# Graph attention on one core: the score products' third runs regrouped over pairs of units

## The chip, the cores and the metric

The kernel runs on one core of one Trainium2 chip. Its time is device microseconds (us) of one execution; the number quoted is the median of several. TensorE (PE, with its weight loads as PEld), VectorE (DVE), ScalarE (ACT), GpSimd (POOL) and SyncE (SP) each run their own queue in order and meet at semaphores.

## The reference, cut to what matters

Two layers, each a graph layer and a mixture of experts, over 1250 nodes of 512 features and 20000 edges. The change is in the first graph layer, an attention with 8 heads of 64 over the edges:

```python
qkv = x @ W
q, k, v = jnp.split(qkv, [Fqk, 2 * Fqk], axis=-1)
aw = jnp.einsum('ehf,ehf->eh', q[src] * scaling, k[dest])
e = jnp.exp(aw - m[src])            # m: maximum over the edges of a source
alpha = e / denom[src]
out = segment_sum(alpha[:, :, None] * v[dest], src)
x = x + out
```

The kernel computes it densely: for each source node the products with all 1250 nodes, plus the logarithm of the number of edges between the two (very negative where there is none), then a softmax over the row.

## The kernel before, in words

The attention runs over 40 units (`UNITS`): 10 tiles of 125 source nodes (`i = u // 4`) times 4 pairs of heads (`j = u % 4`). The order of the work is written out by hand for each engine; semaphores carry counts. For a unit u:

- **Scores** (PE, `scores`, L687; matmul at L696). The 1250 columns are cut in three thirds (`KPIECES`). For each third there is one product for each of the two heads, on rows 0 to 63 and on rows 64 to 127 of the array. Thirds have a running number `g = 3 * u + t`, and third g writes the PSUM bank `2 * h + g % 2`. So it waits until third g - 2 has been taken out (`z_made`).
- **Negated scores** (DVE, `negate_scores`, L1930; L1945). One instruction for a third and head takes the product from PSUM, adds the logarithms, negates, writes `SC[u % 2]`, and carries the minimum along in `neg_max`. The thirds t = 1, 2 read the running minimum; t = 0 starts it. Before t = 0 it waits until the weights of unit u - 2 have been turned.
- **Exponential** (ACT, L1242), one of 1250 columns for each head, when all thirds of the head are there.
- **Turned weights** (PE, `turn_weights`, L699; L707): 20 transposes in 5 blocks of 4. ACT moves blocks 0, 1, 3 from PSUM (L1249), DVE blocks 2 and 4 (`move_block`, L1949; L1952). Three banks take turns as a ring, and a block waits for the move of the block three places back (`release_ring`).
- **Weighed values** (PE, `weigh_values`, L711; L725): 20 products on 64 columns of the array each (40 records), one unit late, into bank 7. ACT moves the result (L1265), PE turns it back a unit later (`turn_output`, L734), and DVE adds it to X (`add_output`, L1966; L1973), which counts `x_added`.

`weigh_values` begins with these waits:

```python
def weigh_values(u):
    above_zero(pe, S("ot_moved"), u)
    above_zero(pe, S("x_added"), 2 * u)
    if tile_at(u + 1, LOGITS_AT) is not None:
        pe.wait_ge(S("log_taken"), tile_at(u + 1, LOGITS_AT) + 1)
```

In unit u PE calls `weigh_values(u - 1)`; the wait is then for `add_output(u - 2)`, which DVE does in unit u behind the negated scores of that unit's first run and its first block move, and PE's part of which (`turn_output(u - 2)`) stands between blocks 2 and 3.

Other work is spread over the units. Row statistics (DVE) in units 5, 9, 13, ...; a normalised row tile turned on PE (L752) in units 6, 10, ...; the routing logits (`route_tile`, PE L762; taken by DVE at L1987) in units 7, 11, ..., 39; ranks (L769, DVE L2002) in units 8, 12, ...; and `out_degree` (DVE, L2079) at the end of the even units 12 to 30. In units 36, 37 and 38 DVE has chains of short instructions (`early_counts`, `early_owners`, `early_done`).

Of the kernel before, what the change touches and what calls it, by code (L numbers as in the profile page):

```python
# [61 lines left out]
UNITS = T * PAIRS  # L62
# [21 lines left out]
def tile_at(u, first):  # L84

    i = (u - first) // PAIRS
    return i if u >= first and (u - first) % PAIRS == 0 and i < T else None


def above_zero(eng, sem, value):  # L90

    if not (isinstance(value, int) and value <= 0):
        eng.wait_ge(sem, value)


def gnn_moe_kernel(nc, x, src, dst, L0_gnn_W, L0_ffn_gate_w, L0_ffn_w1, L0_ffn_w2, L0_ffn_w3,
# [7 lines left out]
    with ExitStack() as ctx:  # L104
# [129 lines left out]
        def bank(b, rows=128, cols=512, off=0):  # L234
            return ps[0:rows, 512 * b + off:512 * b + off + cols]
# [43 lines left out]
        def S(n):  # L279
            return s[n]  # L280
# [230 lines left out]
        def _(pe):  # L511
# [175 lines left out]
            def scores(u, thirds):  # L687

                i, j = u // PAIRS, u % PAIRS
                for t in thirds:  # L690
                    a, z = KPIECES[t]
                    g = 3 * u + t
                    for h in range(2):
                        r = DH * h
                        above_zero(pe, S("z_made"), 2 * (g - 2) + h + 1 if g > 1 else 0)
                        pe.matmul(bank(2 * h + g % 2, P, z - a), QT[r:r + DH, i, j, :],  # L696
                                  KT[r:r + DH, j, a:z], start=True, stop=True).then_inc(S("s_made"), 1)

            def turn_weights(u, blocks):  # L699

                for b in blocks:
                    n = ring_at(u, b)
                    release_ring(n - 3)
                    for k in range(4):
                        h, kt = (4 * b + k) // T, (4 * b + k) % T
                        pe.wait_ge(S("p_made"), 2 * u + h + 1)
                        ins = pe.transpose(bank(4 + n % 3, P, P, k * P), SC[u % 2][h][:, kt * P:kt * P + P],  # L707
                                           ident[0:P, 0:P])
                    ins.then_inc(S("p_turned"), 1)
# [20 lines left out]
            def turn_output(u):  # L730

                pe.wait_ge(S("ot_moved"), u + 1)
                above_zero(pe, S("x_added"), 2 * u)
                pe.transpose(bank(7, P, 128, 256), OT[u % 2], ident[:, :]).then_inc(S("ot_turned"), 1)  # L734
# [6 lines left out]
            def output_bank_free(u):  # L741

                pe.wait_ge(S("ot_moved"), min(u + 1, UNITS))
                pe.wait_ge(S("x_added"), 2 * min(u, UNITS))

            def turn_normed_row(i):

                n = RING_AT[("row", i)]
                release_ring(n - 3)
                pe.wait_ge(S("xn_made"), T + i + 1)  # L750
                for c in range(C):
                    ins = pe.transpose(bank(4 + n % 3, 128, P, c * P), XR[i % 3][:, c * 128:c * 128 + 128],  # L752
                                       ident[0:P, 0:P])
                ins.then_inc(S("xt_turned"), 1)

            def route_tile(i):

                if i == 0:
                    pe.wait_ge(S("gate_in"), 16)
                pe.wait_ge(S("xt_moved"), T + i + 1)  # L760
                for c in range(C):
                    ins = pe.matmul(bank(7, P, E0, 128), XT[:, c, i * P:i * P + P], gate_w[:, c, 0:E0],  # L762
                                    start=c == 0, stop=c == C - 1, skip_group_check=True)
                ins.then_inc(S("log_made"), 1)

            def rank_tile(i):

                pe.wait_ge(S("mask_made"), i + 1)
                pe.matmul(bank(7, 126, 8, 136), before[0:126, 0:126], counted[:, i % 2, :], start=True, stop=True,  # L769
                          skip_group_check=True).then_inc(S("rank_made"), 1)  # L770

            def take_out_counts(k):

                pe.matmul(bank(7, 1, 8, 144), ident[0:126, 125:126], counted[:, k, :], start=True, stop=True,
                          skip_group_check=True).then_inc(S("count_made"), 1)

            for u in range(UNITS):
                if u + 1 < UNITS:
                    scores(u + 1, (0, 1))
                if tile_at(u, LOGITS_AT) is not None:  # L780
                    output_bank_free(u - 2)
                    route_tile(tile_at(u, LOGITS_AT))
                if tile_at(u, RANKS_AT) is not None:
                    output_bank_free(u - 2)
                    rank_tile(tile_at(u, RANKS_AT))
                    if tile_at(u, RANKS_AT) == EARLY_ROWS:
                        take_out_counts(EARLY_ROWS % 2)
                turn_weights(u, range(0, 3))
                if 2 <= u:
                    turn_output(u - 2)  # L790
                turn_weights(u, range(3, BLOCKS))
                if tile_at(u, ROWS_AT) is not None:
                    turn_normed_row(tile_at(u, ROWS_AT))
                if u + 1 < UNITS:
                    scores(u + 1, (2,))
                if 1 <= u:
                    weigh_values(u - 1)

# [923 lines left out]
        def _(dve):  # L1722
# [207 lines left out]
            def negate_scores(u, t):  # L1930

                i, j = u // PAIRS, u % PAIRS
                a, z = KPIECES[t]
                g = 3 * u + t
                if t == 0:
                    if j == 0:
                        dve.wait_ge(logs_in[i % 2], 32 * (i // 2) + 32)
                    above_zero(dve, S("p_turned"), BLOCKS * (u - 1))
                    above_zero(dve, S("rden_made"), 2 * (u - 1))
                for h in range(2):  # L1940
                    dve.wait_ge(S("s_made"), 2 * g + h + 1)
                    least = neg_max[:, 2 * (u % 2) + h:2 * (u % 2) + h + 1]
                    if t:
                        dve.wait_ge(S("z_made"), 2 * (g - 1) + h + 1)
                    dve.tensor_tensor_reduce(SC[u % 2][h][:, a:z], bank(2 * h + g % 2, P, z - a), LNB[i % 2][:, a:z],  # L1945
                                             -1.0, least if t else 3.0e38, ALU.add, ALU.min, least)\
                       .then_inc(S("z_made"), 1)

            def move_block(u, b):  # L1949
                dve.wait_ge(S("p_turned"), BLOCKS * u + b + 1)  # L1950
                above_zero(dve, S("o_made"), u - 1)
                dve.tensor_copy(PT[u % 2][:, 4 * b:4 * b + 4, :],  # L1952
                                bank(4 + ring_at(u, b) % 3, P, 4 * P).rearrange("p (i n) -> p i n", n=P))\
                   .then_inc(S("pt_moved_v"), 1)
# [130 lines left out]
                negate_scores(0, t)  # L2085
            for u in range(UNITS):
                if u + 1 < UNITS:
                    negate_scores(u + 1, 0)
                    negate_scores(u + 1, 1)
                move_block(u, DVE_BLOCKS[0])  # L2090
                if 2 <= u:
                    add_output(u - 2)
                if tile_at(u, LOGITS_AT) is not None:
                    take_logits(tile_at(u, LOGITS_AT))
                if tile_at(u, RANKS_AT) is not None:
                    take_ranks(tile_at(u, RANKS_AT))
                if tile_at(u, STATS_AT) is not None:
                    dve.wait_ge(S("x_added"), 2 * (u - 1))
                    row_stats(X, tile_at(u, STATS_AT))
                inverse_den(u)  # L2100
                if u + 1 < UNITS:
                    negate_scores(u + 1, 2)
                move_block(u, DVE_BLOCKS[1])
                if tile_at(u, STATS_AT) is not None:
                    normed_row(tile_at(u, STATS_AT))
                if tile_at(u, LOGITS_AT) is not None:
                    pick_two(tile_at(u, LOGITS_AT))
                if u >= OUT_DEGREE_AT and u % 2 == 0 and u < OUT_DEGREE_AT + 2 * T:
                    out_degree((u - OUT_DEGREE_AT) // 2)
                if u == RANKS_AT + PAIRS * EARLY_ROWS:  # L2110
                    early_counts()
                if u == RANKS_AT + PAIRS * EARLY_ROWS + 1:
                    early_owners(EARLY_TILES, early_owner, S("slot_made"))
                if u == RANKS_AT + PAIRS * EARLY_ROWS + 2:
                    early_done(EARLY_TILES)
# [414 lines left out]
```

## Time and profile before

| | |
|---|---|
| time, median of 3 | 880.06 us (879.31 to 882.21) |
| time of the profiled execution | 882.13 us |
| its span | 880.4 us |
| PE busy in the span | 828.3 us (94%) |
| attention's units | from 183.60 to about 490 us of the span |

Times in the rows are microseconds from the start of the span, and durations in microseconds unless marked ns. A row of the timeline gives start, duration, engine, line, operation, what is written and read, how many records it merges, and in brackets the idle time of the engine before it and what ended it. A matmul with float32 operands leaves two records.

### The profile page before, as it was taken

The numbers are of one execution on the slowest core, as the hardware profiler recorded it, in microseconds if no ns is written. First come the engines' busy times: TensorE is split into PE (matmuls) and PEld (weight loads), VectorE is DVE, ScalarE is ACT, GpSimd is POOL, SyncE is SP. The second block draws the span as 40 slices with busy tenths as digits, with TensorE's granted clock in tenths as the row PEclk, the third lists the DMA queues.
The fourth block names the chain that finished last, engine by engine and source line by source line (L and its number), as shares of the span: only waits on it lengthen the run. The fifth ranks groups of instructions, "written<-read, shape, count | busy, mean of one in ns | idle before, by whom it ended". The sixth has DMA issues, their size and how long they took to land.

```text
span 880.4 us, 16072 instructions
## 1 busy us (share of the span) xinstructions
PE 828.3 (94%) x5125; PEld 559.6 (64%) x5125; DVE 560.4 (64%) x1839; ACT 374.3 (43%) x680; POOL 207.9 (24%) x381
## 2 busy tenths in 40 slices
PE   5999999899999999999999899999979999996996
PEld 2456555357777777777777676777644445766664
DVE  6489999167878888888877365555552515875111
ACT  1344544366665666666566233343310021543331
POOL 4200000000022022102203342122255511564453
PEclk9999999999999999999999899999999999996999
DMA  9918878896102223110825636554136250185450
GB/s 253 339 29 218 219 203 222 153 320 173 31 25 73 67 80 85 33 51 25 294 95 148 212 96 197 171 168 149 61 108 146 75 179 13 36 265 147 147 173 18
DMA packets 87362, 121.00 MB, mean 137 GB/s; under 512 B 40781, under 2 KB 50157, under 8 KB 87021
## 3 DMA queue, kind: packets, MB, share of 16 engines
q1 hardware_dynamic: 73677, 101.82, 39.7%
q0 software_dynamic: 13600, 18.11, 7.4%
q8 instruction: 46, 0.75, 0.4%
q14 instruction: 39, 0.32, 0.1%
HBM read 65.52 MB, written 57.08 MB: 139 GB/s over the span
## 4 chain that ended last, share of the span: by engine, by line
PE 75%; DVE 9%; DMA 7%; issue 3%; POOL 2%; ACT 2%; SPq 1%; DVEq 0%; POOLq 0%; ACTq 0%
PE ps L806 18%; PE ps L696 11%; PE ps L725 10%; PE ps L707 10%; PE ps L936 7%; PE ps L586 5%; PE ps L963 4%; PE ps L813 4%; DVE R_B L1844 3%; PE ps L591 2%; DVE R_B L1843 2%; DMA R_A<-slots_d 1%; DMA R_B<-slots_d,slot 1%; PE ps L527 1%; DMA R_A<-slots_d,slot 1%
## 5 line engine op out<-in xcount | busy, mean ns | idle before, releaser
L806 PE MATMUL ps<-R_B,R_A 128*128 x612 | 185.7, 446 | 1.7 <-ACT R_A L1418 0.6
L806 PEld LDWEIGHTS ps<-R_B,R_A 128*128 128x128 f32 x612 | 112.0, 194 | 34.8 <-issue 24.5
L1242 ACT ACTIVATE R_A<-R_A,neg_max 125x1250 f32<-125x1250 f32 x80 | 106.6, 1333 | 57.5 <-DVE neg_max L1945 57.5
L696 PE MATMUL ps<-R_B 64*125 64x417 f32 (+1 forms) x480 | 106.5, 544 | 2.5 <-ACT XN L1184 1.5
L1945 DVE CUSTOM_DVE_ANT_0 R_A<-ps,R_B,neg_max 125x417 f32<-125x417 f32 (+1 forms) x160 | 97.6, 648 | 15.0 <-PE ps L696 15.0
L707 PEld LDWEIGHTS ps<-ident,R_A 125*125 125x125 f32 x800 | 93.7, 188 | 14.2 <-issue 13.3
L707 PE MATMUL ps<-ident,R_A 125*125 125x125 f32 x800 | 102.3, 277 | 0.0
L725 PEld LDWEIGHTS ps<-R_W,XN 125*64 125x64 f32 x1600 | 85.3, 136 | 23.6 <-issue 23.6
L725 PE MATMUL ps<-R_W,XN 125*64 125x125 f32 x1600 | 94.7, 272 | 0.5 <-DVE X L1973 0.5
L1249 ACT ACTIVATE R_W<-ps 125x500 f32<-125x500 f32 x120 | 66.1, 585 | 47.8 <-PE ps L707 47.8
L586 PE MATMUL ps<-XT,R_W 128*128 128x500 f32 (+1 forms) x192 | 72.4, 522 | 0.6 <-ACT XT L1167 0.6
L1945 DVE CUSTOM_DVE_ANT_0 R_A<-ps,R_B 125x417 f32<-125x417 f32 x80 | 44.2, 590 | 44.7 <-PE ps L696 31.2
L1844 DVE TENSOR_SCALAR R_B<-R_B 125x418 bf16<-125x418 uint16 x180 | 69.2, 384 | 0.0
L813 PEld LDWEIGHTS ps<-ident,R_A 128*128 128x128 f32 x306 | 38.7, 143 | 34.5 <-issue 20.3
L1952 DVE COPY R_W<-ps 125x500 f32<-125x500 f32 x80 | 54.0, 675 | 9.0 <-PE ps L707 8.7
L696 PEld LDWEIGHTS ps<-R_B 64*125 64x125 f32 x480 | 39.6, 183 | 30.1 <-issue 21.6
L813 PE MATMUL ps<-ident,R_A 128*128 128x128 f32 x306 | 49.9, 279 | 7.5 <-DMA R_A<-slots_d 3.6
L1578 POOL TENSOR_TENSOR rms<-ssum,half_pow 128x1 f32<-128x1 f32 x54 | 30.0, 557 | 102.5 <-DVE ssum L2125 67.8
L1843 DVE TENSOR_SCALAR R_B<-R_B 125x125 bf16<-125x125 uint16 x180 | 45.1, 250 | 13.6 <-PE ps L527 13.2
L586 PEld LDWEIGHTS ps<-XT,R_W 128*128 128x128 f32 x192 | 36.9, 196 | 25.4 <-issue 23.7
L527 PE MATMUL ps<-R_B 125*125 125x418 bf16 x180 | 43.6, 351 | 6.8 <-DVE R_B L1844 5.0
L1554 POOL IOTA R_B<- 125x4 int32 x2 | 0.3, 148 | 196.3 <-DVE mv L1752 196.3
(272 smaller groups left out, 1151.0 us busy)
## 6 DMA issues: line engine op xcount, KB each, us to landing
slots_d<-R_B SPq DMA_DIRECT2D x9, 2322.0 KB, 12.2
R_B<-in_L_ffn_w_dram SPq DMA_DIRECT2D x28, 512.0 KB, 6.8
R_A<-slots_d SPq DMA_DIRECT2D x27, 256.0 KB, 2.8
slots_d<-R_A SPq DMA_DIRECT2D x27, 256.0 KB, 2.5
counts_d<-R_A SPq DMA_DIRECT2D x10, 546.9 KB
logs_d<-R_B SPq DMA_DIRECT2D x10, 546.9 KB
R_B<-logs_d SPq DMA_DIRECT2D x10, 546.9 KB
R_B<-counts_d SPq DMA_DIRECT2D x10, 546.9 KB
```

What stands on the lines that cost most here:

```text
L586: ins = pe.matmul(b[:, 0:z - a], Wqkv[:, c, w:w + 128], XT[:, c, a:z], start=c == 0, stop=c == C - 1)
L696: pe.matmul(bank(2 * h + g % 2, P, z - a), QT[r:r + DH, i, j, :], KT[r:r + DH, j, a:z], start=True, stop=True).then_inc(S("s_made"), 1)
L707: ins = pe.transpose(bank(4 + n % 3, P, P, k * P), SC[u % 2][h][:, kt * P:kt * P + P], ident[0:P, 0:P])
L725: ins = pe.matmul(ps[r:r + DH, 512 * 7:512 * 7 + P], XN[:, kt, (2 * j + h) * DH:(2 * j + h) * DH + DH], PT[u % 2][:, T * h + kt, :], start ...
L806: ins = pe.matmul(bank(b, TM, width), lhs[:, c * TM:c * TM + TM], flat[:, bass.ds(e * (n * width) + c * width, width)], start=c == 0, stop ...
L813: ins = pe.transpose(bank(b, 128, TM, c * TM), source[:, c * 128:c * 128 + 128], ident[:, :])
L936: return pe.matmul(bank(b, 128, z - a), HS[i][:, c * 128:c * 128 + 128], counts_of[i][:, a:z], start=i == 0, stop=i == T - 1)
L1242: act.activation(SC[u % 2][h], SC[u % 2][h], ACT.Exp, bias=neg_max[:, 2 * (u % 2) + h:2 * (u % 2) + h + 1], scale=-1.0, accum_out=den[:, 2 ...
L1249: act.activation(PT[u % 2][:, 4 * b:4 * b + 4, :], bank(4 + ring_at(u, b) % 3, P, 4 * P).rearrange("p (i n) -> p i n", n=P), ACT.Copy).the ...
L1843: dve.tensor_scalar(oh_dst[:, slot, :], iota_dst, win[:, 0, w:w + 1], None, ALU.is_equal)
L1844: return dve.tensor_scalar(hot_of[:, slot, 0:width], iota_src[:, 0:width], win[:, 1, w:w + 1], win[:, 2, w:w + 1], ALU.is_equal, ALU.mult)
L1945: dve.tensor_tensor_reduce(SC[u % 2][h][:, a:z], bank(2 * h + g % 2, P, z - a), LNB[i % 2][:, a:z], -1.0, least if t else 3.0e38, ALU.add, ...
```

## The change

Every unit had two score runs on PE: at its top thirds 0 and 1 of the next unit, and behind its turned weights third 2 of the next unit. Now an even unit u does thirds 0 and 1 of unit u + 1 at its top, and behind its turned weights third 2 of unit u + 1 and third 0 of unit u + 2. An odd unit u does thirds 1 and 2 of unit u + 1 at its top and has no second run. DVE's order follows: in an even unit third 0 of unit u + 2 is negated behind block 4, and in an odd unit nothing is negated between `inverse_den` and block 4. The order of the thirds, and what each waits for, are as before.

```diff
             for u in range(UNITS):
                 if u + 1 < UNITS:
-                    scores(u + 1, (0, 1))
+                    scores(u + 1, (1, 2) if u % 2 else (0, 1))
...
                 turn_weights(u, range(3, BLOCKS))
...
-                if u + 1 < UNITS:
+                if u + 1 < UNITS and u % 2 == 0:
                     scores(u + 1, (2,))
+                if u + 2 < UNITS and u % 2 == 0:
+                    scores(u + 2, (0,))
                 if 1 <= u:
                     weigh_values(u - 1)
...
                 if u + 1 < UNITS:
-                    negate_scores(u + 1, 0)
-                    negate_scores(u + 1, 1)
+                    negate_scores(u + 1, 1 if u % 2 else 0)
+                    negate_scores(u + 1, 2 if u % 2 else 1)
                 move_block(u, DVE_BLOCKS[0])
...
                 inverse_den(u)
-                if u + 1 < UNITS:
+                if u + 1 < UNITS and u % 2 == 0:
                     negate_scores(u + 1, 2)
                 move_block(u, DVE_BLOCKS[1])
+                if u + 2 < UNITS and u % 2 == 0:
+                    negate_scores(u + 2, 0)
```

## Rows read from the trace of the kernel before

**Rows 1.** The page's first part: busy time, share of the span, instructions.
```profile
PE 828.3 (94%) x5125; PEld 559.6 (64%) x5125; DVE 560.4 (64%) x1839; ACT 374.3 (43%) x680; POOL 207.9 (24%) x381
```
**Rows 2.** Chain that ended last, unit 25 of the attention: start, duration, what.
```profile
403.39 1.60 PE ps L696 x8
404.99 1.50 PE ps L707 x12
406.50 0.11 PE ps L734
406.61 0.87 PE ps L707 x8
407.48 0.90 PE ps L696 x4
408.38 2.30 PE ps L725 x39
```
**Rows 3.** Busy time by stretch, unit 25: PE, PEld, DVE, ACT, POOL; clock, DMA share, GB/s at the end.
```profile
403.32:410.60 7.28, 7.28 (x75) 5.47 (x73) 7.02 (x22) 4.29 (x7) 2.22 (x4) 1.00 0.29 73
```
**Rows 4.** Timeline, unit 25: PE's first run and DVE up to the added output.
```profile
403.32 1.67 PE L696 MATMUL ps<-R_B 64*125 64x417 f32 x8
...
404.46 0.59 DVE L1945 CUSTOM_DVE_ANT_0 R_A<-ps,R_B 125x417 f32<-125x417 f32 x1 [0.15 <-PE ps L696]
...
405.49 0.65 DVE L1945 CUSTOM_DVE_ANT_0 R_A<-ps,R_B,neg_max 125x417 f32<-125x417 f32 x1
...
406.64 0.67 DVE L1952 COPY R_W<-ps 125x500 f32<-125x500 f32 x1
...
407.23 0.47 DVE L1973 SCALAR_TENSOR_TENSOR X<-ps,rden,X 125x64 f32<-125x64 f32 x2
```
**Rows 5.** Who waited for the added output, whole span: us, times.
```profile
PE ps L725: 0.5, 1
```
**Rows 6.** Timeline, unit 39, which has no score run in the kernel before.
```profile
482.20 1.39 PEld L707 LDWEIGHTS ps<-ident,R_A 125*125 125x125 f32 x12
...
484.47 0.47 DVE L1973 SCALAR_TENSOR_TENSOR X<-ps,rden,X 125x64 f32<-125x64 f32 x2
484.85 0.16 DVE L1987 COPY R_B<-ps 125x8 f32<-125x8 f32 x1
...
485.22 2.37 PE L725 MATMUL ps<-R_W,XN 125*64 125x125 f32 x40 [0.45 <-DVE X L1973]
```
**Rows 7.** Timeline, the attention's start: DVE's third 2 of unit 1, then PE.
```profile
188.68 0.65 DVE L1945 CUSTOM_DVE_ANT_0 R_A<-ps,R_B,neg_max 125x416 f32<-125x416 f32 x1 [0.93 <-PE ps L696]
...
189.40 0.29 PEld L696 LDWEIGHTS ps<-R_B 64*125 64x125 f32 x2 [0.72 <-DVE neg_max L1945]
...
190.92 1.55 PEld L707 LDWEIGHTS ps<-ident,R_A 125*125 125x125 f32 x12 [0.66 <-DVE R_W L1952]
```
**Rows 8.** Timeline, unit 27, which routes a tile.
```profile
420.89 1.39 PEld L707 LDWEIGHTS ps<-ident,R_A 125*125 125x125 f32 x12
...
424.27 1.81 PEld L725 LDWEIGHTS ps<-R_W,XN 125*64 125x64 f32 x34 [0.60 <-issue]
```
**Rows 9.** Timeline, unit 24, which sums an out degree on DVE.
```profile
400.13 0.97 PE L696 MATMUL ps<-R_B 64*125 64x416 f32 x4
...
401.12 0.65 DVE L1945 CUSTOM_DVE_ANT_0 R_A<-ps,R_B,neg_max 125x416 f32<-125x416 f32 x1 [0.35 <-PE ps L696]
...
402.86 1.44 DVE L2079 TENSOR_REDUCE deg_out<-R_B 125x1 f32<-125x1250 f32 x1
```
**Rows 10.** Timeline, unit 38: PE's first run, DVE's first third, the turned row.
```profile
472.34 1.67 PE L696 MATMUL ps<-R_B 64*125 64x417 f32 x8
...
474.22 0.59 DVE L1945 CUSTOM_DVE_ANT_0 R_A<-ps,R_B 125x417 f32<-125x417 f32 x1
...
477.12 0.65 PE L752 MATMUL ps<-ident,R_B 125*128 125x125 f32 x4 [0.62 <-DVE R_W L1952]
```

## The prediction

> **What bounds the kernel now.** I read the page's busy times first, then the chain that ended last, then the timeline of single units. TensorE is busy for 94% of the span [rows 1]; that only says where to look. The chain shows what sets the pace of the attention: through unit 25 it runs on PE alone, from score products to turned weights, the turned output, the second score run and the weighed values, with no other engine and no wait in it [rows 2]. The period is 1.60 + 1.50 + 0.11 + 0.87 + 0.90 + 2.30 = 7.28 us. PE is busy in all 7.28 us of that stretch, at a granted clock of 1.00 (the 2.4 GHz level), but DVE is busy in 7.02 of them [rows 3]. So PE sets the end, and DVE follows it with little in hand. This is the number to remember: a change that shifts work to or from one side of a wait can make DVE's order the bound though its total is smaller.
>
> **What a score run costs.** A run of two thirds took 1.60 us and a run of one third 0.90 [rows 2]. The difference, 0.70, is a third itself; the rest, 0.20, is paid once a run. Before, units 0 to 38 hold 39 runs of each kind. Afterwards, over units 0 to 37, each pair of units has three runs of two thirds: 4.80 us against 2 x 1.60 + 2 x 0.90 = 5.00. There are 19 such pairs (units 38 and 39 do the same as before), and as many instructions as before on every engine. If nothing else moved, the gain would be 19 x 0.20 = 3.8 us.
>
> The Trainium skill (TensorE: Matmul & The Clock Gate, section Single matmul latency) gives a part of a lone matmul that does not depend on its columns, 166 ns at the full clock. By the rows a run's fixed part is 0.20 us; by the page, taken as that part, it would be an estimate of 19 x 0.166 = 3.2 us instead of 3.8. Both are gains, and neither decides the sign.
>
> **Where the run was, and what it covered.** The even unit gets 0.70 us longer on PE (a third more in its second run). The odd unit loses its second run, 0.90 us, if PE can go straight from the turned weights to the weighed values. It can't, because `weigh_values(u - 1)` waits for `x_added` of `add_output(u - 2)`, which DVE does in the same unit behind four negated scores and a block move. I put both on one scale, from T, the start of the first run.
>
> - PE, before: the turned weights are through at T + 4.09 and the weighed values begin at T + 4.99; the 0.90 between is the second run [rows 2].
> - DVE, before: first negation at T + 1.14, added output from T + 3.91 to T + 4.38 [rows 4]. That is 0.29 us after PE is through with the weights, and nobody notices: in the whole span PE waited for the added output once, for 0.5 us [rows 5].
> - DVE, after: the first product comes no sooner, so the start is again T + 1.14. The four negations are now thirds 1 and 2, all with the running minimum. Such a pair took 406.64 - 405.49 = 1.15 us, the pair of third 0 took 405.49 - 404.46 = 1.03 [rows 4]; so 0.12 more. The added output ends at T + 4.50.
>
> The cover that hid this was the second run itself. The one time that PE waited is unit 39, the one late odd unit without a second run in the kernel before. There the added output started at 484.47, ended at 484.94, and the weighed values began at 485.22, PE having idled 0.45 us for it [rows 6]. That is 0.28 behind DVE's end; between them DVE also took out the logits until 485.01, which this unit waits for too. A plain unit has no such step. The bounds of the way from DVE's end to PE's start are 0.07 us (a product released by a negation: 188.68 + 0.65 to 189.40 [rows 7]) and 0.28. I take 0.18, since the wait is followed by the same further waits of `weigh_values` as in unit 39, less the logits.
>
> **The sum**, on the span, in groups of pairs:
>
> - Plain odd units: 3, 5, 9, 13, ... 37, ten of them (the row statistics stand behind the added output, so they change nothing). Weighed values at T + 4.50 + 0.18 = T + 4.68 against T + 4.99: the odd unit gets 0.31 shorter and the even one 0.70 longer. Net +0.39 each, +3.9. With 0.07 and 0.28 it is +2.8 and +4.9.
> - Odd units with routing: 7, 11, ... 35, eight. There PE has the logits' products before the turned weights, DVE waits for block 2, and unit 39 is the direct precedent: 482.20 to 485.22, 3.02 us from the first turned block to the weighed values [rows 6], against 3.38 in unit 27 [rows 8]. So 0.36 back, 0.70 paid, +0.34 each, +2.7.
> - `out_degree`. In unit 24, DVE went from the second run's start 400.13 to the reduction at 402.86 and needed 1.44 more, until 404.30 [rows 9], just before the next first product at 404.46 [rows 4]. Now 1.03 us of third 0 of unit u + 2 stand ahead of it, while PE's next unit starts only 0.70 later, so DVE is 1.03 - 0.70 - 0.16 = about 0.17 late into the odd unit. That adds to the stall in units 13, 17, 21, 25, 29, and something like it in 37 after the early counts: +1.0. In routing units it disappears, since DVE waits for block 2 there. Where DVE had more in hand it is 0.
> - The first pair. Unit 1 has no `x_added` to wait for, and saves its 0.90. But at the start the runs meet with no weighed values between them, and third 2 of unit 2 waits until third 0 of unit 2 has been negated: from 188.68, two negations (1.15), a move (0.59, as from 406.64 to 407.23 [rows 4]) and two more (1.03) are 191.45, plus 0.07 and its own 0.90 make 192.4, against turned weights at 190.92 [rows 7]. So +1.5 - 0.9, some of it cover for other small waits: +0.5 (0 to 1).
> - Unit 38. DVE enters it late, first third at 474.22, 1.88 behind PE's 472.34 instead of 1.14, and PE waited 0.62 for the bank of the turned row [rows 10]. Unit 37 now has no third 2 to negate (1.15 less on DVE, and PE's stall gives it more time), which takes this wait away: -0.7 to 0; I take -0.7.
>
> Together +3.9 + 2.7 + 1.0 + 0.5 - 0.7 = +7.4 us. ACT is no bound: the exponential of unit u + 1 starts no later against PE's next weights than before (its third 2 is ready earlier in odd units, and in even units PE's longer run gives 0.70 more). The logarithms' loads and the expert weights that SP issues on counts of scores are half a unit nearer to their use, and no wait for them shows after the start. Behind the attention the order is unchanged and passes the delay on.
>
> The profiled execution took 882.13 us with a span of 880.4, so its sum is 889.5; it lies 2.07 above the median of 880.06, and I set the forecast against the median: 887.5 us, 0.84% slower.
>
> **The rivals.**
>
> *The wait is not there in time to matter, and the 0.20 is kept.* Then 880.06 - 3.8 = 876.3. It speaks for it that DVE waits 0.15 for the first product in unit 25 [rows 4] and has 1.15 us less to do in the odd unit. But that work stood behind the added output, not ahead of it, and the start is bound by the product itself. It decides if the added output is through before T + 4.09; with the way to PE it would need 0.6 us less ahead of it. Chance 0.06.
>
> *The run's fixed part doesn't go with the run.* The 0.20 could belong to any change between turned weights and weighed values, paid with or without scores between them. With the stall in place this is hidden inside it, so the forecast stands; without it the result is 880.06 within a microsecond. That, with stalls small enough to cancel the gain, is the case of no difference (under 0.3%, 2.6 us, about what a measurement of this kernel can tell from no change). Chance 0.07.
>
> *VectorE becomes the bound in the even units.* It gets eight negations there, 2 x 1.03 + 2 x 1.15 = 4.4 us, and its moves. If its lateness isn't made good in the odd unit but runs on in the ten pairs with `out_degree`, at a further 0.3 to 0.5 us each, 3 to 5 us come on top: about 892. Against it: the odd unit loses what the even one gains, and each stall of PE is time for DVE. Chance 0.10. The Trainium skill (TensorEngine Tiling, section PSUM Bottleneck) says that tiling speeds up TensorE but not taking the results out of PSUM, and that the copies may become the limit. By the rows here it is the copies' place in the order that does it, and not their sum.
>
> **How the numbers follow.** The forecast (stall at the added output, about +7.4) has 0.77. Its range: 0.07 everywhere, no lateness and no cost at the start give 2.8 + 2.7 - 0.7 = +4.8, 884.9; 0.28, a start of 1.0, lateness in all and unit 38's gain lost give 4.9 + 2.7 + 1.0 + 1.0 = +9.6, 889.7. Some of the third rival and the spread of the runs (0.3%) come on top, so 883.0 to 891.0. Slower: 0.77 + 0.10 = 0.87; same 0.07; faster 0.06.
>
> **What would show it.** In the profile after: in odd units no L696 between L707 and L725, and instead a wait of L725 for DVE's L1973, 18 times, each some 0.4 to 0.6 us; even second runs of 1.60 us; the pair of units 24 and 25 about 0.4 to 0.6 longer than before; the wait of L752 in unit 38 gone. The prediction is wrong if L725 follows L707 in odd units with no wait, if DVE's first negation there comes well before T + 1.14, or if time appears outside the attention.

## The result and the profile after

The changed kernel takes 886.27 us (median of 7, 882.48 to 889.15) against 880.71 (7 runs, 878.95 to 882.21). The ratio is 1.0065, with a 95% interval of 1.0043 to 1.0087: 0.65% slower, some 5.7 us, where 7.4 were forecast. The profiled execution has a span of 887.4 us.

First the page's busy time of the kernel after, to hold against [rows 1].

```profile
PE 828.9 (93%) x5125; PEld 564.4 (64%) x5125; DVE 559.4 (63%) x1839; ACT 373.2 (42%) x680; POOL 209.6 (24%) x381
```

PE has the same instructions and, over the whole span, nearly the same busy time. That hides two things, which the span cut in two shows: the attention (from unit 1's first score run to the start of the weighed values in unit 39), then all behind it. The columns are those of [rows 3]; the first two lines are of the kernel before, the others of the kernel after:

```profile
183.60:485.19 301.59, 300.10 (x2952) 227.63 (x2953) 243.67 (x804) 187.80 (x323) 45.79 (x112) 1.00 0.34 102
485.19:880.40 395.21, 366.32 (x1559) 243.15 (x1559) 182.81 (x543) 112.31 (x236) 148.18 (x225) 0.97 0.43 131
```

```profile
182.73:489.31 306.58, 297.99 (x2952) 229.91 (x2952) 242.33 (x804) 186.71 (x323) 46.06 (x112) 1.00 0.33 99
489.31:887.40 398.09, 369.04 (x1559) 245.65 (x1559) 183.14 (x543) 112.28 (x236) 149.63 (x225) 0.96 0.44 130
```

In the attention PE is busy 2.1 us less, but idle 8.6 us instead of 1.5. Behind it PE is busy 2.7 us more with as many records, at a lower mean clock; that part comes back below.

Where PE waits shows in the chain that ended last, here of units 28 and 29 (start, duration, what), to be held against [rows 2]:

```profile
403.30 1.60 PE ps L696 x8
404.90 2.30 PE ps L725 x40
407.20 1.60 PE ps L696 x8
408.80 1.50 PE ps L707 x12
410.30 0.11 PE ps L734
410.41 0.87 PE ps L707 x8
411.28 0.51 issue
411.80 2.37 PE ps L725 x40
```

A word on the numbers of units. Counted in the trace by the weighed values (L725), the stretches that are called units 24, 25 and 27 in the rows and in the prediction are of units 28, 29 and 31, one tile later. Those are units of the same kinds with the same periods (7.50, 7.28 and 8.15 us before), so no sum changes. From here on units go by this count.

The even unit's second run is now 1.60 us. In the odd unit none stands between the turned weights (through at 411.28, 4.08 after the first run's start) and the weighed values, but a gap of 0.51 does. The chain calls it "issue". A plain odd unit, unit 3, shows on the timeline what ends it (the last field is the idle time before):

```profile
204.36 1.67 PE L696 MATMUL ps<-R_B 64*125 64x417 f32 x8
...
205.36 0.65 DVE L1947 CUSTOM_DVE_ANT_0 R_A<-ps,R_B,neg_max 125x417 f32<-125x417 f32 x1 [1.06 <-PE ps L696]
...
207.66 0.67 DVE L1954 COPY R_W<-ps 125x500 f32<-125x500 f32 x1
...
208.25 0.47 DVE L1975 SCALAR_TENSOR_TENSOR X<-ps,rden,X 125x64 f32<-125x64 f32 x2
...
208.78 2.16 PEld L725 LDWEIGHTS ps<-R_W,XN 125*64 125x64 f32 x40 [0.46 <-issue]
208.81 2.37 PE L725 MATMUL ps<-R_W,XN 125*64 125x125 f32 x40 [0.30 <-issue]
```

The added output ends at 208.72, and the first weights for the weighed values are loaded at 208.78. The list of waits of the kernel after gives the same stall two names (us in total, times, longest); together they are 18 times, once for each odd unit from 3 to 37, and 7.4 us:

```profile
PE ps L725 <- issue: 4.2, 10, 0.5
...
PE ps L725 <- DVE X L1975: 3.2, 8, 0.4
```

To compare units, I take the period of unit u as the time from the start of the weighed values (first weight load of L725) in unit u - 1 to that in unit u. In us, with the kernels of the experiments beside it:

| period of | before | after | e1 | e2 | e3 | e4 | e5 | e9 |
|---|---|---|---|---|---|---|---|---|
| 3 (plain odd) | 7.28 | 6.72 | 6.39 | 7.28 | 7.31 | 7.33 | 6.72 | 6.38 |
| 4 (plain even) | 7.28 | 8.01 | 7.98 | 7.28 | 8.01 | 7.31 | 8.01 | 8.37 |
| 13 (odd behind an out degree) | 7.28 | 6.94 | 6.38 | 7.29 | 7.53 | 7.32 | 6.72 | 6.39 |
| 27 (odd with routing) | 8.15 | 7.69 | 7.26 | 8.16 | 8.28 | 8.28 | 7.69 | 7.26 |
| 28 (even, ranks) | 7.50 | 8.24 | 8.20 | 7.50 | 8.23 | 7.53 | 8.23 | 8.59 |
| 14 (even, turned row) | 7.81 | 8.54 | 8.51 | 7.81 | 8.54 | 7.84 | 8.77 | 8.80 |
| 38 | 8.55 | 8.15 | 8.56 | 8.44 | 8.16 | 9.10 | 8.16 | 7.93 |

From unit 3 on the units of a kind agree within 0.05 us in each kernel, but for units 35 to 38, which have work of their own, unit 24 of e4 (7.62), and in e5 units 6, 10 and 34, which turn a row with no out degree ahead of it (8.54, where 14 has 8.77). This grain is far finer than the times of whole executions, which spread over some us.

### The profile page after: what moved, and what is told of

The parts are those of the page before. It is cut to its first block, busy times and chain, and to the rows that moved or that the text cites. A ratio compares the mean times of both kernels' runs of the same rounds, so it can differ in the third digit from the quotient of the medians.

```text
span 887.4 us, 16071 instructions
## 1 busy us (share of the span) xinstructions
PE 828.9 (93%) x5125; PEld 564.4 (64%) x5125; DVE 559.4 (63%) x1839; ACT 373.2 (42%) x680; POOL 209.6 (24%) x381
## 4 chain that ended last, share of the span: by engine, by line
PE 73%; DVE 10%; DMA 7%; issue 4%; POOL 2%; ACT 2%; SPq 1%; DVEq 0%; POOLq 0%; ACTq 0%
PE ps L808 18%; PE ps L696 10%; PE ps L725 10%; PE ps L707 9%; PE ps L938 6%; PE ps L586 5%; PE ps L965 4%; PE ps L815 4%; DVE R_B L1846 3%; PE ps L591 2%; DVE R_B L1845 2%; DMA R_A<-slots_d 2%; PE ps L527 1%; DMA R_B<-slots_d,slot 1%; DMA R_A<-slots_d,slot 1%
## 5 line engine op out<-in xcount | busy, mean ns | idle before, releaser
L696 PE MATMUL ps<-R_B 64*125 64x417 f32 (+1 forms) x480 | 102.2, 536 | 1.7 <-ACT XN L1186 1.5
L725 PE MATMUL ps<-R_W,XN 125*64 125x125 f32 x1600 | 94.8, 272 | 7.9 <-issue 4.2
L725 PEld LDWEIGHTS ps<-R_W,XN 125*64 125x64 f32 x1600 | 85.8, 136 | 22.6 <-issue 22.5
L696 PEld LDWEIGHTS ps<-R_B 64*125 64x125 f32 x480 | 41.5, 183 | 33.6 <-issue 24.4
```

The lines of the kernel that those rows point to most:

```text
L725: ins = pe.matmul(ps[r:r + DH, 512 * 7:512 * 7 + P], XN[:, kt, (2 * j + h) * DH:(2 * j + h) * DH + DH], PT[u % 2][:, T * h + kt, :], start ...
```

## The experiments

### e1: the added output ahead of the block move

```diff
-                move_block(u, DVE_BLOCKS[0])
+                if u % 2 == 0:
+                    move_block(u, DVE_BLOCKS[0])
                 if 2 <= u:
                     add_output(u - 2)
                 if tile_at(u, LOGITS_AT) is not None:
                     take_logits(tile_at(u, LOGITS_AT))
+                if u % 2:
+                    move_block(u, DVE_BLOCKS[0])
```

> The changed kernel, but in odd units DVE adds the output (and takes the logits) before it moves block 2, so x_added comes 0.59 us sooner; the same instructions, one place earlier. Theory A (the gain is lost in the wait for the added output, set by what stands ahead of it on DVE): added output from about T + 3.4 to T + 3.9 after the first run's start, before the turned weights are through at T + 4.09, so L725 follows L707 without a wait in odd units. Odd periods go from 6.72 (6.94 after an out degree, 7.69 with routing) to about 6.38 (6.38, 7.25): 4 x 0.34 + 6 x 0.55 + 8 x 0.44 = 8.2 us faster than the changed kernel, 3 us faster than the kernel before. Theory B (the run's fixed 0.20 us belongs to the switch from turned weights to weighed values and stays): odd periods no shorter than about 6.58, and the kernel before is only just reached. Theory C (DVE's amount of work is the bound): no different from the changed kernel.

Measured: 0.9958 of the kernel before (0.9936 to 0.9980), so faster than both kernels. The timeline of its unit 3:

```profile
203.90 1.67 PE L696 MATMUL ps<-R_B 64*125 64x417 f32 x8
...
207.22 0.48 DVE L1975 SCALAR_TENSOR_TENSOR X<-ps,rden,X 125x64 f32<-125x64 f32 x2
207.62 0.67 DVE L1954 COPY R_W<-ps 125x500 f32<-125x500 f32 x1
...
207.99 1.06 PEld L725 LDWEIGHTS ps<-R_W,XN 125*64 125x64 f32 x20
```

With T the start of the unit's first run, the added output is through at T + 3.80, and the weights' load follows at T + 4.09 with no idle time before it. The odd periods up to unit 37 are 6.38 to 6.39, with routing 7.25 to 7.26, as expected to 0.01 us. They are 0.90 shorter than before, the whole of the missing run, and even ones are 0.70 longer. That is the gain of 0.20 a pair that the change could bring and didn't. It also throws out theory B: turned weights pass to weighed values with no cost of their own. And theory C: DVE has exactly as much to do.

### e2: the same exchange in the kernel before

The edit of e1, made in the kernel before.

> The kernel before with the same exchange on DVE in odd units (added output before block 2). Theory A: nothing, within 0.3%, since the second run covers the added output there either way; the periods stay 7.28 in plain units. Theory C: also nothing. If this alone made the kernel some us faster, the gain of the exchange in the changed kernel would not be evidence for A.

Measured: 0.9988 (0.9968 to 1.0009), no difference, and periods as before up to unit 37. The exchange is worth nothing where a score run covers the added output. Unit 39 is the one late odd unit without such a run in the kernel before, and there it is worth 0.47 us: 6.60 becomes 6.12, here and in e1 alike. Unit 38 got 0.11 shorter, and the last weighed values start 0.15 later behind unit 39.

### e3 and e4: 0.59 us more ahead of the added output

```diff
             for u in range(UNITS):
...
+                if u % 2 and u > 2:
+                    dve.wait_ge(S("p_turned"), BLOCKS * u + 3)
+                    dve.tensor_copy(R_A[0:P, 5100:5600].rearrange("p (i n) -> p i n", n=P), bank(4 + ring_at(u, 2) % 3, P, 4 * P)
+                                    .rearrange("p (i n) -> p i n", n=P))
                 move_block(u, DVE_BLOCKS[0])
```

In the kernel after (e3) and in the kernel before (e4).

> The changed kernel with one more copy of block 2 (125 x 500, to a place that nobody reads) on DVE ahead of the move of block 2 in odd units from 3 on: 0.59 us more ahead of the added output. Theory A: each of the 18 or 19 waits grows by 0.59, so about 10.6 us slower than the changed kernel (odd plain period 6.72 to 7.31). Theory C (amount of DVE work, averaged): less, since DVE has over 1 us a pair idle. If the wait is for something else, nothing up to about 2 us.

> The kernel before with the same added copy in odd units. Theory A: the second run covers it, up to its 0.9 us: the added output is through at T + 4.97 in plain units, against weighed values at T + 4.99, so 0.0 to 0.1 there, and about 0.15 in the nine routing units: 1 to 4 us slower than before in all. Theory C: about as much as in the changed kernel, some 10 us.

Measured: e3 1.0186 (1.0157 to 1.0215), e4 1.0023 (1.0006 to 1.0041), both against the kernel before. Against the kernel after, e3 is 1.0186 / 1.0065 = 1.012, some 10.6 us for 19 copies of 0.59. Every odd period grew by 0.59, from 6.72 to 7.31, from 6.94 to 7.53, from 7.69 to 8.28. In the kernel before, the same copies made plain odd units 0.05 longer and routing units 0.13. Unit 38 grew by 0.54, and unit 39, which has no second run to cover them, by the whole 0.59. So what stands ahead of the added output passes to the end one for one in the changed kernel, and hardly at all in the one before: its second run had some 0.54 us in hand for it.

### e5, e6 and e8: the out degrees in odd units

```diff
-                if u >= OUT_DEGREE_AT and u % 2 == 0 and u < OUT_DEGREE_AT + 2 * T:
+                if u > OUT_DEGREE_AT and u % 2 and u < OUT_DEGREE_AT + 2 * T:
                     out_degree((u - OUT_DEGREE_AT) // 2)
```

e5 is this in the kernel after, e6 is this with the exchange of e1. The reason lies in units 28 and 29 of the kernel after, on the timeline, against [rows 9]:

```profile
405.97 0.58 DVE L1947 CUSTOM_DVE_ANT_0 R_A<-ps,R_B 125x417 f32<-125x417 f32 x1
406.47 0.58 DVE L1947 CUSTOM_DVE_ANT_0 R_A<-ps,R_B 125x417 f32<-125x417 f32 x1
...
406.99 1.45 DVE L2081 TENSOR_REDUCE deg_out<-R_B 125x1 f32<-125x1250 f32 x1
407.13 0.29 PEld L696 LDWEIGHTS ps<-R_B 64*125 64x125 f32 x4 [0.17 <-DVE neg_max L1947]
...
408.35 0.64 DVE L1947 CUSTOM_DVE_ANT_0 R_A<-ps,R_B,neg_max 125x417 f32<-125x417 f32 x1
```

DVE takes the first product 1.22 after the run's start instead of 1.00, since the reduction is still at work, and unit 29 takes 6.94 instead of 6.72.

> The changed kernel with out_degree at the end of the odd units 13 to 31 in place of the even ones 12 to 30. Theory A with DVE's lateness as a term of its own: units 13, 17, 21, 25, 29 fall from 6.94 to 6.72 like the others, 1.1 us in all. But the reduction now stands behind the normalised row in odd units that precede a turned row, and 1.44 us there put DVE's start in the next even unit at about the first product or 0.1 late; the turned row on PE waits for block 2's bank with nothing in hand, so up to 0.1 each may come back in units 14, 18, 22, 26, 30. Net 0.6 to 1.1 us faster than the changed kernel, still slower than before. If lateness were not a term of its own, nothing would change.

> The changed kernel with the added output ahead of block 2 in odd units and out_degree in odd units. With the exchange the lateness is already hidden (odd periods 6.38 either way), so A expects no gain from the second edit here: like the kernel with the exchange alone, or up to 0.5 us slower by the turned rows. If the lateness reached PE by another way than the added output, this would be 1 us faster than the exchange alone.

Measured: e5 1.0083 (1.0053 to 1.0113), e6 1.0063 (1.0041 to 1.0085). Both expectations missed on the total. The part that was asked for came out: units 13, 17, 21, 25 and 29 fell to 6.72. But units 14, 18, 22, 26 and 30 rose from 8.54 to 8.77 (forecast: up to 0.1), and in e6 from 8.51 to 9.02. There the turned row (L752) waits for block 2's bank, which DVE now moves later: 0.11 us in e5, and 0.38 in e6, where PE arrives 0.34 sooner. The wait isn't the whole price in e5: behind it the turned row takes 0.65 in the chain instead of 0.53. And unit 35 took 9.90 in e5 and 12.56 in e6, against 7.69 and 7.26. In e6 the waits name it (waits, then the timeline with SP's issue of the load):

```profile
DVE R_A L1947 <- DMA R_B<-logs_d: 3.2, 1, 3.2
```

```profile
439.61 1.58 SPq L327 DMA_DIRECT2D R_B<-logs_d  x2
...
451.17 0.59 DVE L1947 CUSTOM_DVE_ANT_0 R_A<-ps,R_B 125x417 f32<-125x417 f32 x1 [3.22 <-DMA R_B<-logs_d]
```

DVE wants the logarithms of tile 9 for third 0 of unit 36, which the change had brought from unit 35 into unit 34. SP issues that load behind the weights of the experts, and those wait for the last out degree, which the edit had put back from unit 30 to 31. Two steps, each of half a unit or one, used up a margin that no wait of the kernel before shows. Two other rows show it, SP's issue of that load and DVE's first use of it, 20 us apart there:

```profile
430.08 2.87 SPq L327 DMA_DIRECT2D R_B<-logs_d  x2
...
450.32 0.59 DVE L1945 CUSTOM_DVE_ANT_0 R_A<-ps,R_B 125x417 f32<-125x417 f32 x1 [1.51 <-PE ps L696]
```

In e6 the use follows 11.6 us behind the issue, and only after its wait. e8 tests it: e5 with that load ahead of the weights.

```diff
             load_logs(8)
+            load_logs(9)
             sp.wait_ge(S("deg_out_made"), T)
...
             for e in range(3):
                 load_w1e(e)
-            load_logs(9)
```

> The changed kernel with out_degree in odd units, as in e5, and SP's load of the logarithms of tile 9 issued ahead of the expert weights instead of behind eleven of them. If the extra 2.2 us of unit 35 in e5 are the wait for this load (its queue is held by the last out degree, which e5 moved one unit back, and its first use came half a unit nearer), unit 35 goes from 9.90 back to 7.69 and DVE shows no wait for it. The other units stay as in e5: odd after an out degree 6.72, units 14, 18, 22, 26, 30 at 8.77. If unit 35 stays long, the cause is another.

Measured: unit 35 at 7.70, no wait for the logarithms after the first, all other units as in e5. From the start of unit 1's weighed values to that of the last ones (in the call behind unit 39) the attention takes 300.19 us, in e5 302.35, in the kernel after 300.12. So the cause of unit 35's extra time in e5 is shown, and also that moving the out degrees gains nothing: 5 x 0.22 off and 5 x 0.23 on. Its whole time, 1.0082 (1.0057 to 1.0107), doesn't tell it from e5; 2.2 us are inside these intervals.

### e7: a chain of short instructions one unit later

e1 with `early_owners` in unit 38 instead of 37.

> The changed kernel with the exchange, and with early_owners (seven short DVE instructions, 1.44 us) in unit 38 in place of unit 37. The wait of the turned row (L752) in unit 38 is then gone: period 8.56 to about 7.9, 0.6 us faster than the exchange alone. It can be lost again if the first expert tiles, whose addresses come from early_owners, are loaded later than PE needs them; the load was issued some 11 us ahead of its use, so I expect no loss.

Measured: 0.9976 (0.9957 to 0.9995), not faster than e1. Unit 38 did fall, from 8.56 to 7.81, more than expected. What was expected of the loads was wrong: the first three row tiles were issued at 478.75 instead of 472.97, all else in SP's queue stands behind them, and the waits of PE's weight loads for rows, past the attention, went from the first to the second of these rows (e1, then e7):

```profile
PEld ps L815 <- DMA R_A<-slots_d: 4.9, 3, 2.7
```

```profile
PEld ps L815 <- DMA R_A<-slots_d: 8.6, 3, 3.7
```

That is 3.7 us given back for 0.75 gained, in these two executions. I didn't try the chain elsewhere.

### e9: one run more, and nothing else

e1, with the even units' second run split in two runs of one third.

```diff
                 turn_weights(u, range(0, 3))
+                if u + 1 < UNITS and u % 2 == 0:
+                    scores(u + 1, (2,))
                 if 2 <= u:
                     turn_output(u - 2)
                 turn_weights(u, range(3, BLOCKS))
...
-                if u + 1 < UNITS and u % 2 == 0:
-                    scores(u + 1, (2,))
                 if u + 2 < UNITS and u % 2 == 0:
                     scores(u + 2, (0,))
```

> The kernel with the exchange (e1), but with the even units' second run split: third 2 of unit u + 1 ahead of the turned output, third 0 of unit u + 2 behind the turned weights; so four runs a pair again, and no new wait. Theory A with a price of 0.20 us for a run: even periods 0.20 longer than in e1 (8.20 to 8.40), odd ones the same 6.38, 7.26; 3.8 us in all, level with the kernel before. Theory B (the 0.20 hangs on the switch to the weighed values): no difference from e1.

Measured: 1.0007 (0.9990 to 1.0024), level with the kernel before, as expected. But the price is not 0.20. Against e1, even periods grew by 0.39 (0.29 with a turned row), and the odd ones not at all but for unit 37 (0.16). Unit 38 gave 0.63 back, as its turned row no longer waits. So the total alone would have passed for a price of 0.20. The chain of its unit 4, and then the same stretch in e1:

```profile
212.79 1.50 PE ps L707 x12
214.29 0.90 PE ps L696 x4
215.19 0.30 PE ps L734
215.49 0.87 PE ps L707 x8
216.37 0.90 PE ps L696 x4
```

```profile
211.96 1.50 PE ps L707 x12
213.46 0.11 PE ps L734
213.57 0.87 PE ps L707 x8
```

Each run of one third is again 0.90, so 0.20 for the run, as forecast; the turned output behind it went from 0.11 to 0.30. A run's price is 0.20 where weighed values follow, and 0.39 in these plain even units. The Trainium skill (TensorEngine Tiling, section Key Properties) says that a change of tiling mode drains TensorE. The 0.20 and 0.19 here fit that for the change between 64-row products and full transposes, though no row shows a drain as such; between turned weights and weighed values, which use the array at 128 by 64, e1 shows no such cost, and there the measurement decides.

## Why the prediction was right, step by step

- **PE sets the pace, DVE follows closely.** Right (e3 against e4).
- **A run costs 0.20, 19 runs fewer are 3.8 us.** Right as a price: e1, without the stall, has even periods 0.70 longer and odd ones 0.90 shorter than before, 3.6 us in 18 pairs. The first pair doesn't pay it back (0.30 longer, below), and 0.47 in unit 39 comes from the exchange alone, as e2 shows; that the sum of these is again 3.7 us, and e1 0.42% faster, is chance.
- **The second run covered the added output, and the cover goes.** Right, in 18 odd units. This step decides the sign, and e1 to e4 together show it. The stalls are 0.30 us in four units (3, 5, 9, 33), 0.40 in the eight routing units and 0.49 to 0.52 in the six late ones; the prediction had 0.4 to 0.6.
- **Plain odd units, +0.39 a pair.** Too much by 0.21: units 3 and 4 take 14.74 us together against 14.56, +0.18. Two sizes in it were too large, 0.26 in all. From DVE's end to PE's start I took 0.18, from unit 39 [rows 6]; it was 0.06, at the foot of the range [rows 7]. In unit 39 the logits, which DVE takes last, stand between; in unit 31 of the kernel after, which takes them too, PE starts 0.24 behind the added output and still 0.17 behind the logits, and why that is more than 0.06 no run shows. And the first negation starts at T + 1.00, not T + 1.14: the 1.14 of [rows 4] belongs to third 0, and third 1 is taken 0.14 sooner. I kept the start and changed only the durations, though the late run of [rows 9] had 0.99 in plain sight. A first negation well before T + 1.14 was named as a sign of being wrong; it came 0.14 before, which made the stall smaller and didn't take it away. A third size was too small: the even unit behind a stall got 0.73 longer, not 0.70. Without the stall, in e1, it is 0.70; in the chain of the kernel after, the weighed values that follow a stall take 2.37 instead of 2.30.
- **Routing units, +0.34.** Measured -0.46 + 0.73 = +0.27.
- **DVE's lateness behind an out degree, 0.17.** Measured 0.22, and 0.19 in unit 37; shown by e5, where it goes.
- **The first pair, +0.5.** Measured from the first score run of unit 1 to its weighed values: 11.05 before, 11.35 after, +0.30.
- **Unit 38, -0.7.** Measured -0.40: of the turned row's wait of 0.62, 0.19 stayed.

From unit 1's first run to the start of the weighed values in unit 39 the attention is 5.0 us longer (forecast 7.4), 2.0 of the difference in the plain units with their lateness. That 5.0 is what the working has to answer for. The 5.7 us of the whole executions has an interval of 3.8 to 7.7, so it agrees with 5.0, and that it lies nearer to the forecast is no merit of the working.

The part behind is 2.9 us longer in the profiled executions, 398.1 against 395.2, with no edit there, and the attention began 0.87 us sooner; 5.0 + 2.9 - 0.9 is the 7.0 us between the spans. Time outside the attention was a sign of being wrong, so it needs a reading. PE's busy time makes up 2.7 of the 2.9, for the same number of records, while the mean granted clock was 0.96 instead of 0.97. The profiled execution is also the slowest of the seven, 889.15 us, with a clock of 0.978 over its span, where the other six had 0.984 to 0.986 and the profiled one of the kernel before 0.984. Over all eleven profiles PE's busy time in this part by and large goes with the clock: 364.5 us at a mean of 0.973 in e1, 366.3 at 0.969 before, 368.4 at 0.960 in e9, 369.0 at 0.956 after. The part as a whole varied by 5 us, from 393.2 to 398.2, in the ten kernels that share it (all but e7). So this is most likely the clock of one execution and not the change; why the clock was lower in it stays open, and no run tests it.

The rivals: the one with the gain kept failed at the place named. The run's fixed part does go with the run. VectorE as the bound of even units did not occur here, but the waits of 0.11 and 0.38 us in e5 and e6 show how near it is.

## What to carry to other kernels

Work between two waits is also cover. Before taking a piece of PE's work from one place to another, put both engines on one scale from a common start, and see what the next wait is for and when that is done; here 0.29 us of lateness had been hidden by a run of 0.90. When the cover goes, look at what stands ahead of the release in the other queue and doesn't belong there: one exchange of two steps on DVE turned 0.65% slower into 0.42% faster. Then read the queues that such an edit brings nearer to their use, the loads above all, since a margin that suffices leaves no wait; it has to be read from issue to first use.

## What the runs showed that I had not expected

- A stall behind a semaphore can appear as "issue". Ten of the eighteen stalls did, those of the units without routing, where DVE had ended 0.06 us before PE's next start.
- After the long wait of unit 35 in e6 the granted clock fell, by the stretches of that kernel (PE, PEld, DVE, ACT and POOL busy, clock, DMA share, GB/s):

```profile
435.00:445.00 10.00, 10.00 (x100) 8.09 (x96) 8.78 (x29) 7.04 (x13) 0.97 (x3) 1.00 1.05 356
445.00:455.00 10.00, 8.17 (x68) 5.45 (x67) 5.53 (x19) 3.61 (x6) 0.00 (x0) 0.93 0.78 194
455.00:465.00 10.00, 10.00 (x80) 8.63 (x80) 4.26 (x18) 4.76 (x9) 0.81 (x3) 0.73 0.14 49
```

  PE had waited in the second stretch, and a mean of 0.73 in the third says that part of it ran at 1.2 GHz instead of 2.4. DVE's wait of 3.2 us made the unit 5.3 us longer. The wait of 2.8 us at the same place in e5 and the eighteen short stalls of the changed kernel, 0.3 to 0.5 us each, left the clock at 1.00.
- One transposition behind a score run took 0.30 us instead of 0.11 in the chain, so the same split costs twice what the run's own rows say (e9).
